# The residual copies of a group moved behind the transposed copies of a later group on ScalarE

## What is computed

```python
sel = jax.nn.sigmoid(xt @ expert_sel.T)
sel_val, sel_idx = jax.lax.top_k(sel, TOP_K)
w = jnp.zeros((T, E), dtype=xt.dtype).at[jnp.arange(T)[:, None], sel_idx].add(sel_val)
h = jax.nn.relu(jnp.einsum('td,edh->teh', xt, keys))        # keys (32, 256, 64)
out = jnp.einsum('teh,te,ehv->tv', h, w, values)            # values (32, 64, 256)
t = t + out                                                 # xt = normalised t
```

## Time and profile before

| | us |
|---|---|
| median of 3 runs | 443.06 |
| lowest and highest of them | 438.97, 445.83 |
| the profiled execution | 436.99 |
| its span, first to last instruction | 435.2 |

### The profile page before, as it was taken

How to read it: one execution, slowest core, us unless ns; L and a number is a source line. 1 busy time by engine, 2 the same in 40 slices (tenths; PEclk the granted TensorE clock), 3 DMA queues, 4 the chain that set the end, 5 groups by cost and what they waited for, 6 DMA issues and landing times. The chain is left out here.

```text
span 435.2 us, 10495 instructions
## 1 busy us (share of the span) xinstructions
PE 372.2 (86%) x2982; PEld 282.5 (65%) x2982; DVE 331.1 (76%) x1032; ACT 272.3 (63%) x817; POOL 286.7 (66%) x377
## 2 busy tenths in 40 slices
PE   8989999999999999999999998867879998865000
PEld 2756787786778787678878787632667777664000
DVE  2874788897789898789999998678478999997010
ACT  1333677775777767677787887670759998935000
POOL 6334536877677876687788888774466777777600
PEclk9999999999999999999999999975999999999655
DMA  7999421132123111122211211122779777532397
GB/s 202 366 206 188 133 52 50 49 109 96 57 66 101 57 51 56 51 73 81 69 62 64 63 56 57 62 76 97 231 244 279 211 215 207 147 103 78 111 237 190
DMA packets 32442, 53.31 MB, mean 123 GB/s; under 512 B 7580, under 2 KB 25454, under 8 KB 31885
## 3 DMA queue, kind: packets, MB, share of 16 engines
q1 hardware_dynamic: 22688, 28.45, 24.8%
q0 software_dynamic: 7488, 21.40, 15.3%
q10 hardware_dynamic: 2208, 2.78, 2.1%
HBM read 30.49 MB, written 24.68 MB: 127 GB/s over the span
## 5 line engine op out<-in xcount | busy, mean ns | idle before, releaser
L1475 PE MATMUL bank<-vT,prob 128*128 128x256 f32 x512 | 116.0, 380 | 1.8 <-POOL prob L612 1.8
L1475 PEld LDWEIGHTS bank<-vT,prob 128*128 128x128 f32 x512 | 95.1, 191 | 14.0 <-POOL prob L612 2.4
L686 POOL DMA_INDIRECT out<-vT,dest x72 | 70.9, 984 | 25.7 <-issue 16.2
L589 POOL DMA_INDIRECT slot_rows<-rows,slot x64 | 65.0, 1015 | 17.1 <-issue 15.3
L612 POOL TENSOR_TENSOR prob<-prob,ginv 128x1024 f32<-128x1024 f32 x32 | 61.2, 1914 | 21.1 <-DVE ginv L1061 21.1
L583 POOL TENSOR_TENSOR rstd<-rstd,half_neg 128x1 f32<-128x1 f32 x64 | 35.7, 558 | 44.7 <-ACT rstd L736 44.4
L797 ACT ACTIVATE prob<-prob 128x1024 f32<-128x1024 f32 x32 | 33.8, 1057 | 20.1 <-DVE prob L1029 20.1
L1025 DVE TENSOR_REDUCE gmax<-X 128x32 f32<-128x1024 f32 x32 | 39.2, 1224 | 7.9 <-PE X L1395 7.8
L1055 DVE TENSOR_REDUCE gsum<-prob 128x32 f32<-128x1024 f32 x32 | 38.8, 1211 | 3.6 <-ACT prob L797 3.5
L1029 DVE TENSOR_TENSOR prob<-X,gmax 128x1024 f32<-128x1024 f32 x32 | 39.2, 1224 | 1.1
L1286 DVE SCALAR_TENSOR_TENSOR vT<-bank,wgt,vT 128x256 f32<-128x256 f32 x72 | 29.9, 477 | 7.6 <-PE bank L1626 5.3
(11 more groups left out here) (235 smaller groups left out, 840.7 us busy)
## 6 DMA issues: line engine op xcount, KB each, us to landing
xt<-x_tok SPq DMA_DIRECT2D x32, 128.0 KB, 2.2
values_s<-values SPq DMA_DIRECT2D x2, 2048.0 KB, 29.0
out<-out POOLq DMA_DIRECT2D x4, 832.0 KB, 14.7
xc_or_xin<-x_cm SPq DMA_DIRECT2D x3, 1024.0 KB, 10.3
xc_or_xin<-slot_rows SPq DMA_DIRECT2D x20, 130.0 KB
t<-slot_rows SPq DMA_DIRECT2D x16, 130.0 KB
keys_s<-keys SPq DMA_DIRECT2D x1, 2048.0 KB, 15.1
t<-slot_rows SPq DMA_DIRECT2D x24, 65.0 KB
```

The lines of the kernel that those rows point to most:

```text
L589: g.indirect_dma_start(out=slots_d, out_offset=bass.IndirectOffsetOnAxis(ap=slot[:, t % RB, r:r + 1], axis=0), in_=rows[:, t % RB, r, :], ...
L686: g.indirect_dma_start(out=out, out_offset=bass.IndirectOffsetOnAxis(ap=dest[:, n % (2 * NB), k:k + 1], axis=0), in_=yb[:, n % NB, k, :], ...
L1475: mm = m.matmul(av_p, pr[:, j, :], vT[:, b % 2, j, :], start=(j == 0), stop=(j == KB - 1))
```

## The change

In iterations 3 to 15 of the loop on ACT, `residual(n)` runs after `load_last_tile(n + 5)` and `transposed(n + 2)` instead of before them. In iterations 16 and 17 neither of these exists, so nothing moves. No instruction is added, removed or altered, and the other engines' programs are the same.

```diff
             for n in range(EARLY, GROUPS):
                 if n + 1 < GROUPS:
                     keys_copied(n + 1)
-                residual(n)
                 if BY_ACT <= n + AHEAD < GROUPS:
                     load_last_tile(n + AHEAD)
                 if n + 2 < GROUPS:
                     transposed(n + 2)
+                residual(n)
```

## The result

| | before | changed |
|---|---|---|
| median of 22 runs, us | 444.88 | 443.71 |
| lowest, highest | 438.97, 449.05 | 441.99, 452.23 |
| the profiled execution | 436.99 | 448.92 |

The ratio of changed to before is 1.0069, 95% interval 1.0044 to 1.0094. It compares only runs within 1.5% of each kernel's fastest, while a median counts all of them; the kernel before has more long runs, and so its median lies above. The change is 0.7% slower like for like (3.1 us), which is inside what counts as the same. Predicted was 446.9 in a range of 441 to 452, within 2% with a chance of 0.87.

What follows compares the result with a forecast made beforehand. POOL's issue rate and DVE's work on groups 15 to 17 were taken to bound the loop's end together. POOL's last send 3.8 us late, nothing for the rest, on the median of 443.06 gave 446.9 us, range 441 to 452.

Steps and rivals of the forecast that it cites:

- POOL and DVE arrive together at the end: End of loop: POOL's issue rate and DVE's work on groups 15 to 17 meet, slack 3.74, 0.10 and 0.19 us.
- The middle costs nothing: Middle of the loop: the copy ahead of the residual costs nothing, thinly covered, with 0.36 us to spare at group 8.
- the second rival: A DMA of 1.88 us before group 10's copy delays group 8's residual; end 5.0 us later, 448.1 us, chance 0.10.
- The residual of group 15 is 3.9 us late at DVE: ACT's residual waits behind group 17's copy and ends at 391.41, so DVE's weighted sum of group 15 starts 3.9 us late.
- POOL's last send is 3.8 us late: POOL at groups 16 and 17: slack hides nearly all at group 15, then sends and the fixed tail come 3.8 us late.
- The clock falls in the longer gap and costs nothing: PE's gap before the outputs of group 16 grows from 1.79 to about 5.7 us; the clock falls but recovers, cost nothing.
- A gap of 3.15 us left the granted clock at 1.00.: PE at 379.1 in the profile before: the clock outlasted this gap at 2.4 GHz; the longer gap to come was expected to lower it.
- The footing: 3.8 us on top of the median of 443.06: Whole kernel: the delay was added to the median of three runs before, giving 446.9 us, 0.9% slower.
- The sum on the profile's own footing, 440.8: Whole kernel: the 3.8 us delay put on the profiled execution of 436.99 us, giving 440.8 us.

Runs made afterwards that it cites:

- the clock kept high: Kernel before and changed kernel, each with warming matmuls in all five gaps of PE at the loop's end: 438.83 us and 442.08 us.
- second profile of the changed kernel: The changed kernel run again with no edit, beside the kernel before: 443.39 us, ratio 1.0031.
- ten warming matmuls: Kernel before and changed kernel, each with ten extra PE matmuls ahead of the outputs of group 15: 440.04 us and 444.95 us.

## Why the prediction was right

- **POOL and DVE arrive together at the end.** Right. With the clock kept high the changed kernel's loss at POOL is two waits, ahead of groups 15 and 16, and from the start of the last send to the end of the span it takes 28.6 us, against 28.5 in the profile before.
- **The middle costs nothing.** Nearly right. With the order changed there alone the time could not be told from before. DVE's waits for ACT in the middle were 0.5 us in the kernel with the clock kept high and 0.66 us in the profile with the order changed in the middle alone. The slip of the second rival did happen in the profiled execution: one DMA issue ahead of a copy took 1.51 us, the copy of group 8 started 1.60 us late and DVE waited 1.29 us for the residual of group 6. It was group 6 and not group 8, where I had worked the slack out.
- **The residual of group 15 is 3.9 us late at DVE.** Right: 3.92 us with the clock high. That iteration 15 carries nearly all of it was shown by changing it alone and by leaving it alone, though in medians of all runs the two are the same and only the runs at the higher mean clock part them. That PE's order is the reason was shown by moving the transposes, which took 2.7 us off the changed kernel and nothing off the kernel before.
- **POOL's last send is 3.8 us late.** Right in size: 4.15 us in the profile with the clock high, of which about 0.5 us is the slip in the middle. In run times it was 3.25 us between the two kernels with the clock kept high, and 3.1 us by the ratio.
- **The clock falls in the longer gap and costs nothing.** Right that it falls, and nearly right on the price. In the second profile of the changed kernel it fell there, the outputs of group 16 took 3.68 us, the clock was back for the hidden layer of group 17, and DVE took the weighted sum of group 16 without a wait. But DVE was ready for that hidden layer sooner than it came, and POOL waited 0.54 us for group 17; in the first profile it was 1.12 us and with the ten warming matmuls 1.17 us, against 0.30 with the clock kept high. So the fall cost 0.2 to 0.9 us.
- **"A gap of 3.15 us left the granted clock at 1.00."** True of that execution and wrong as a reading. In five of the profiles above a gap of 2.6 to 3.1 us at the same place was followed by the low clock within 1.4 us, and in one, that of the kernel before run again, 2.63 us left it high. This was the uncertainty that mattered, and the prediction did not have it.
- **The footing: 3.8 us on top of the median of 443.06.** This is the step that did not hold; the changed kernel's median is 443.71, and with the median of all 22 runs of the kernel before, 444.88, the same sum would have given 448.7. The profiled execution of 436.99 had the clock high, and 439.1 is the median of the kernel before in runs with a mean clock of 0.940 or more. The median of the runs already held a part for low clock. That part and the late residual do not add up in full. In runs of the kernel before, those with a mean clock under 0.935 have a median 5 to 8 us above those with 0.940 or more in each of the three sets; in runs of the changed kernel it is 4.4 us in the first 22 and 0.4 us in the twelve of the run again. One reason can be read: a low clock on the hidden layer of group 17 cost the kernel before 3.3 us at POOL (3.58 less 0.30), while the changed kernel, whose DVE is late anyway, paid 0.2 to 0.9 us for the low clock in its new gap. That this is all of it is not shown. Between runs at the higher mean clock the change costs 3.6 us, close to the 3.8 forecast. The sum on the profile's own footing, 440.8, is about as far below the measured median (2.9 us) as the forecast is above it (3.2 us). That 446.9 stands so near is in part luck, and the measured median lies in the range because the range was as wide as the spread of the runs.

## What to carry to other kernels

Moving work behind a wait on one engine was priced here where that wait was longest: look at the last iterations too, where program orders differ from the steady state, and not only at the middle. Where two chains end together, a delay on one is only hidden by the slack at that very place (3.74 us for group 15, 0.10 us for group 16). A wait at the end of such a chain does not name its cause: POOL's 3.60 us ahead of group 16 stood in profiles of both kernels. A median and one profiled execution can stand on different footings; before a cost is added to a median, find out what spreads the runs.

## What the runs showed of the hardware

The granted clock of PE falls in or behind a gap in some executions and not in others of the same length: 3.15 us left it high, 3.14 us was followed by 20 us at 0.50. Once low, it stayed so through 10.00 us in which PE was never idle (384.6 to 394.6, with the new order in iterations 3 to 14). It also fell after a shorter one, in the kernel before with its warming matmuls: PE waited 2.19 us for rows of group 12, and the hidden layer of group 11 that followed took 3.27 us where 1.95 us is usual there; from 355.9 to 359.2 the mean granted clock was 0.56.

```profile
354.96 1.09 PE L1582 MATMUL X<-ident,t 128*128 128x128 f32 x8 [2.19 <-DMA t<-slot_rows]
355.89 3.27 PE L1599 MATMUL X<-prob,k_s 128*128 128x128 f32 x16
```

One program on one core ran between 437 and 448 us on one chip, and 10 or 32 matmuls of no use, about 0.22 us each, narrowed that to 437 to 442.5. Late rows have a share in that spread beside the clock, and how large it is was not measured.
